# The end of an eight-tile transformer kernel, tile pairs 4-5 and 6-7 handled one after the other

## The reference

```
x = x + attn_a(layernorm(x));  x = x + moe(layernorm(x))
x = x + attn_b(layernorm(x));  x = x + moe(layernorm(x))
x = x + attn_c(layernorm(x));  x = x + ffn(layernorm(x))
x = x + latent_attention(layernorm(x));  x = x + ffn(layernorm(x))
```

```
logits = x @ W_gate.T                       # 8 experts, the top 2 are taken
shared = relu(x @ W_up.T) @ W_down.T
out    = shared + sum(softmax(top2)) * (x @ W_expert)
```

## Time and profile before

| what | value |
|---|---|
| time, median of 3 runs | 1894.64 us (1893.88 to 1895.35) |
| profiled execution, its own time | 1893.86 us |
| its span in the trace | 1892.1 us |
| TensorE busy | 1802.4 us, 95% |
| VectorE busy | 1070.0 us, 57% |
| ScalarE busy | 910.9 us, 48% |
| GpSimd busy | 694.6 us, 37% |
| mean granted TensorE clock | 0.986 of full speed |

### The profile page before, as it was taken

The page is one execution under the profiler, slowest core; times in us unless marked ns, Lnnn a source line. Parts: engine busy times, 40 slices in busy tenths (PEclk is TensorE's granted clock), DMA queues, the critical chain, the costliest instruction groups (busy, mean ns, idle before and its releaser), DMA issues. The chain is left out here.

```text
span 1892.1 us, 30184 instructions
## 1 busy us (share of the span) xinstructions
PE 1802.4 (95%) x10570; PEld 1242.4 (66%) x10580; DVE 1070.0 (57%) x1854; ACT 910.9 (48%) x1938; POOL 694.6 (37%) x627
## 2 busy tenths in 40 slices
PE   6999999999999899999999999899998999999998
PEld 3333688888887555788888887423334677887776
DVE  6776444444445665444444445788864676556544
ACT  3677533333333566433333333468874456445431
POOL 5200466666665110466666664600001345211200
PEclk9799999999999999999999999999999999999999
DMA  4400344444440320354444440490001000000000
GB/s 127 123 1 1 86 121 117 113 112 112 112 102 16 87 81 2 98 125 101 117 116 113 116 123 1 108 181 4 1 1 23 1 1 2 1 1 1 1 12 12
DMA packets 137931, 121.77 MB, mean 64 GB/s; under 512 B 84545, under 2 KB 122905, under 8 KB 137593
## 3 DMA queue, kind: packets, MB, share of 16 engines
q1 hardware_dynamic: 137817, 120.24, 25.5%
HBM read 111.41 MB, written 8.65 MB: 63 GB/s over the span
## 5 line engine op out<-in xcount | busy, mean ns | idle before, releaser
L1418 DVE TENSOR_TENSOR e_inner_lo<-e_inner,e_inner_hi 128x512 fp32r<-128x512 f32 x192 | 244.1, 1271 | 379.2 <-ACT e_inner_hi L1381 379.0
L1404 POOL TENSOR_TENSOR e_wsilu<-e_silu,e_rw 128x512 f32<-128x512 f32 x192 | 262.0, 1364 | 204.3 <-ACT e_silu L1375 186.4
L1351 PE MATMUL psum<-e_x_hi,e_w_hi 128*128 128x512 f32 x768 | 302.5, 394 | 4.7 <-DVE e_inner L1426 4.7
L1351 PE MATMUL psum<-e_x_hi,e_w_lo 128*128 128x512 f32 x768 | 299.2, 390 | 0.0
L1351 PE MATMUL psum<-e_x_lo,e_w_hi 128*128 128x512 f32 x768 | 298.9, 389 | 0.0
L1375 ACT ACTIVATE e_silu<-psum 128x512 f32<-128x512 f32 x192 | 114.7, 597 | 342.6 <-PE psum L1351 342.6
L1413 POOL TENSOR_TENSOR e_w_lo<-e_raw,e_w_hi 128x384 fp32r<-128x384 f32 x180 | 221.1, 1229 | 133.5 <-ACT e_w_hi L1392 121.9
L1351 PEld LDWEIGHTS psum<-e_x_hi,e_w_hi 128*128 128x128 f32 x768 | 144.1, 188 | 44.6 <-DVE e_inner L1426 15.6
L1088 DVE TENSOR_REDUCE c_mx<-psum 128x1 f32<-128x1024 f32 x128 | 150.6, 1219 | 27.4 <-PE psum L957 26.9
L1351 PEld LDWEIGHTS psum<-e_x_hi,e_w_lo 128*128 128x128 f32 x768 | 144.2, 188 | 30.5
L1351 PEld LDWEIGHTS psum<-e_x_lo,e_w_hi 128*128 128x128 f32 x768 | 144.2, 188 | 29.1
(11 more groups left out here) (354 smaller groups left out, 3171.6 us busy)
## 6 DMA issues: line engine op xcount, KB each, us to landing
e_rw<-e_rw_dram SPq DMA_DIRECT2D x56, 384.0 KB, 5.1
e_rw<-e_rw_dram SPq DMA_DIRECT2D x56, 256.0 KB, 5.4
e_raw<-in_L_ffn_w_gate SPq DMA_DIRECT2D x64, 192.0 KB, 2.6
e_raw<-in_L_ffn_w_up SPq DMA_DIRECT2D x64, 192.0 KB, 2.6
e_raw<-in_L_ffn_w_down SPq DMA_DIRECT2D x32, 384.0 KB, 3.6
e_rw<-e_rw_dram SPq DMA_DIRECT2D x72, 128.0 KB, 4.7
e_rw<-e_rw_dram SPq DMA_DIRECT2D x16, 192.0 KB, 3.0
c_parts_dram<-c_part SPq DMA_DIRECT2D x8, 384.0 KB, 2.5
```

Of the source, the lines that this page charges most:

```text
L1351: last = nc.tensor.matmul(bank[u % 2][:], self.w[a][s][:, KC * which + k, j * P:(j + 1) * P], self.x[b][:, k, h * HALF:(h + 1) * HALF], st ...
L1404: self.core.nc.gpsimd.tensor_tensor(self.wsilu[:, u % 2, :], self.silu[:, u % 2, :], self.rw[s][:, j, h * HALF:(h + 1) * HALF], ALU.mult). ...
L1418: self.core.nc.vector.tensor_tensor(self.inner_parts[1][:, u % 3, :], self.inner[:, u % 2, :], self.inner_parts[0][:, u % 3, :], ALU.subtr ...
```

## The change

The work of the end is split by tile pairs.

- In step (15, 6), `invert_part` (VectorE), `inverse_part` (TensorE) and `copy_inverse_part` (ScalarE) handle the inverse row sums of tiles 4 and 5, and VectorE stores the contexts of these two tiles. `values` of step (15, 6) waits for that store.
- `last()` begins with the eighth pair of tiles 4 and 5. It ends with the transposition of their normed rows, ahead of the last `inverse` and `values`. Their residual add and norm stand in VectorE's stream ahead of the last context store, which is now 256 columns wide.
- After the last `values` come up, the eighth pair of tiles 6 and 7, up, route and share. The second pair's turn, route, up and share follow.
- 20 zero matmuls become 4; the 3 others stay. Relu is ScalarE's alone, and banks are given out anew. `hT[1]` moves from `xn` to the spent rotary tables in `xi`.

```diff
@@ LatentAttend @@
+    PART_STEP = (UNITS - 1, HT + 1)
+    def inverse_part(self, pe):
+        key, m = "inverse part", self.PART_STEP[0]
+        pe.wait_ge(self.part_inverted, 2)
+        self.bank_free(pe, key)
+        for t in range(2):
+            last = self.core.nc.tensor.transpose(self.turn_bank(key)[:, t * P:(t + 1) * P], ...
+        last.then_inc(self.turned, 1)
     def values(self, pe, m, t, g):
+        if g == 0 and (m, t) == (self.PART_STEP[0], self.PART_STEP[1] + 1):
+            pe.wait_ge(self.ctx_copied, m + 1)
...
+        if (m, t) == self.PART_STEP:
+            self.inverse_part(pe)
         if t % self.HT == self.HT - 1:
             self.inverse(pe, m)
...
+    def invert_part(self, dve):
+        nc.vector.reciprocal(self.inv_one[:, 0:2, :], self.sums[:, m % 2, 0:2, :]).then_inc(self.part_inverted, 1)
+        dve.wait_ge(self.part_inverted, 1)
+        nc.vector.tensor_copy(self.inv[:, m % 2, 0:2, :, :], ...).then_inc(self.part_inverted, 1)
@@ Second.tensor @@
         def last():
-            latent_out.clear(pe, banks["out"][1])
+            for t in (4, 5):
+                latent_out.project(pe, t, side, range(LPAIRS - 1, LPAIRS), True)
+            latent_out.clear(pe, banks["out"])
             for t in (6, 7):
-                latent_out.project(pe, t, banks["out"][1], range(LPAIRS - 1), True)
+                latent_out.project(pe, t, banks["out"], range(LPAIRS - 1), True)
+            norm.turn_pair(pe, 2, 1, 0, banks["turn"][0])
         latents.tensor(pe, before_part, between, behind, last)
-        for t in range(4, 8):
-            latent_out.project(pe, t, banks["out"][t // 2 - 2], range(LPAIRS - 1, LPAIRS), True)
-        keep_warm(20)
-        norm.turn(pe, 2, 1, banks["turn"])
+        norm.wait_pair_stored(pe, 2, 1, 0)
+        ffn2.up_pair(pe, 2, 0, banks["up"][0])
+        for t in (6, 7):
+            latent_out.project(pe, t, banks["out"], range(LPAIRS - 1, LPAIRS), True)
+        ffn2.up_pair(pe, 2, 1, banks["up"][1])
+        for t in (4, 5):
+            ffn2.route(pe, t, banks["route"][0][t % 2])
+        ffn2.share(pe, 2, banks["share"][0])
+        keep_warm(4)
+        norm.turn_pair(pe, 2, 1, 1, banks["turn"][1])
         keep_warm(3)
-        norm.wait_stored(pe, 2, 1)
-        for m in range(2):
-            ffn2.up(pe, 1, m, banks["up"][m])
-        for t in range(4, 8):
-            ffn2.route(pe, t, banks["route"][t - 4])
-        for n in range(2, 4):
-            ffn2.share(pe, n, banks["share"][n - 2])
+        norm.wait_pair_stored(pe, 2, 1, 1)
+        for t in (6, 7):
+            ffn2.route(pe, t, banks["route"][1][t % 2])
+        for m in range(2):
+            ffn2.up_pair(pe, 3, m, banks["up"][m])
+        ffn2.share(pe, 3, banks["share"][1], 4)
@@ Second.scalar @@
+        latents.scalar(act, behind, lambda: norm.store_pair(act, core.nc.scalar.copy, 2, 1, 0, 0, banks["turn"][0][0]))
+        for m in range(2):
+            ffn2.relu_pair(act, relu, 2, m, banks["up"][m])
+        norm.store_pair(act, core.nc.scalar.copy, 2, 1, 1, 0, banks["turn"][1][0])
+        ffn2.exp(act, 2)
+        ffn2.relu_pair(act, relu, 3, 0, banks["up"][0])
+        ffn2.exp(act, 3)
+        ffn2.relu_pair(act, relu, 3, 1, banks["up"][1])
@@ Second.vector @@
+        def norm_of_pair(p, bank):      # add, gather x2, spread_pair, invert_pair, scale_pair
...
+        latents.vector(dve, behind, before_store)   # before_store: norm_of_pair(0), store(0)
+        norm_of_pair(1, banks["out"])
+        store(1)
+        ffn2.sort(dve, 2, routed)
+        add_routed(2)
+        ffn2.sort(dve, 3, routed)
+        for t in (4, 5):
+            ffn2.add_shared(dve, t, banks["share"][0])
+        add_routed(3)
+        for t in (6, 7):
+            ffn2.add_shared(dve, t, banks["share"][1])
```

More of the change, by code:

```diff
@@ L275, in scale, with pair, spread_pair @@
                                 ALU.subtract, ALU.mult).then_inc(self.normed_v, 1)
+    def pair(self, h, p):
+        return range(4 * h + 2 * p, 4 * h + 2 * p + 2)
+    def spread_pair(self, dve, r, h, p):
+        nc = self.core.nc
+        tiles = self.pair(h, p)
+        for t in tiles:
+            dve.wait_ge(self.gathered[h], 4 * r + t % 4 + 1)
+            nc.vector.bn_aggr(self.mv[:, t, :], self.stats[:, t, :]).then_inc(self.aggregated, 1)
+        dve.wait_ge(self.aggregated, 4 * self.place(r, h) + 2 * p + 2)
+        nc.vector.tensor_scalar(self.var[:, 0, tiles.start:tiles.stop], self.mv[:, tiles.start:tiles.stop, 1], self.EPS, None, ALU.add
+                                ).then_inc(self.varied, 1)
@@ new lines, in scale_pair, with turn_pair @@
+    def scale_pair(self, dve, r, h, p):
+        core = self.core
+        dve.wait_ge(self.inverted, self.place(r, h) + p + 1)
+        for t in self.pair(h, p):
+            core.nc.vector.tensor_scalar(core.xn[:, t, :], core.x[:, t, :], self.mv[:, t, 0:1], self.inv[:, 0, t:t + 1],
+                                         ALU.subtract, ALU.mult).then_inc(self.normed_v, 1)
+    def turn_pair(self, pe, r, h, p, banks):
+        core = self.core
+        for t in self.pair(h, p):
+            pe.wait_ge(self.normed_v, 4 * self.place(r, h) + t % 4 + 1)
+            for k in range(KC):
+                last = core.nc.tensor.transpose(core.bank[banks[k]][:, t % 2 * P:(t % 2 + 1) * P], core.xn[:, t, k * P:(k + 1) * P],
+                                                core.ident[:])
+        last.then_inc(self.turned, 1)
@@ L277, in keep, with store_pair, wait_pair_stored @@
+    def store_pair(self, engine, copy, r, h, p, k, bank):
+        c = h * HALF + p * 2 * P
+        engine.wait_ge(self.turned, self.place(r, h) + p + 1)
+        copy(self.core.xT[:, k, c:c + 2 * P], self.core.bank[bank][:, 0:2 * P]).then_inc(self.copied[k], 1)
+    def wait_pair_stored(self, engine, r, h, p):
+        for k in range(KC):
+            engine.wait_ge(self.copied[k], self.place(r, h) + p + 1)
     def keep(self, t):
@@ L1521, in up, with up_pair, relu_pair, share @@
         last.then_inc(self.up_ready, 1)
-    def share(self, pe, n, bank):
+    def up_pair(self, pe, n, m, bank):
         nc, core = self.core.nc, self.core
-        pe.wait_ge(self.relued[n // 2], 2)
+        for k in range(KC):
+            last = nc.tensor.matmul(core.bank[bank][:, 0:2 * P], core.wup[:, k, m * P:(m + 1) * P],
+                                    core.xT[:, k, 2 * n * P:(2 * n + 2) * P], start=(k == 0), stop=(k == KC - 1))
+        last.then_inc(self.up_ready, 1)
+    def relu_pair(self, engine, relu, n, m, bank):
+        engine.wait_ge(self.up_ready, 2 + 2 * (n - 2) + m + 1)
+        relu(self.hT[1][:, m, n % 2 * 2 * P:(n % 2 + 1) * 2 * P], self.core.bank[bank][:, 0:2 * P]).then_inc(self.relued[1], 1)
+    def share(self, pe, n, bank, relued=2):
+        nc, core = self.core.nc, self.core
+        pe.wait_ge(self.relued[n // 2], relued)
         for t in (2 * n, 2 * n + 1):
@@ L1926, in __init__ @@
                     self.turns[m, t, g, a] = len(self.turns)
+            if (m, t) == self.PART_STEP:
+                self.turns["inverse part"] = len(self.turns)
             if t % HT == HT - 1:
@@ L2167, in invert @@
             dve.wait_ge(self.turned, self.turns["inverse", m - 2] + 1)
+        if m == self.PART_STEP[0]:
+            dve.wait_ge(self.turned, self.turns["inverse part"] + 1)
         nc.vector.reciprocal(self.inv_one[:], self.sums[:, m % 2, :, :]).then_inc(self.inv_made, 1)
@@ L2188, in back @@
                 self.rotate(dve, *part)
-            if t % self.HT == self.HT - 1:
+            if (m, t) == self.PART_STEP:
+                self.store(dve, m, "inverse part", t, slice(0, 2 * P))
+            if (m, t) == self.steps[-1]:
+                before_store()
+                self.store(dve, m, tiles=slice(2 * P, HALF))
+            elif t % self.HT == self.HT - 1:
                 self.store(dve, m)
@@ L2931 @@
               "up0": 12, "up1": 13, "ex0": 13, "ex1": 14, "share0": 14}
-    LAST_BANKS = {"out": (7, 0), "turn": (2, 3), "route": (4, 5, 6, 1), "up": (2, 3), "share": (0, 7)}
+    LAST_BANKS = {"out": 0, "turn": ((1, 2), (6, 7)), "route": ((1, 2), (6, 7)), "up": (3, 5), "share": (4, 0), "zeros": 3}
     def __init__(self, core, c, first_norm, latent):
@@ L3262, in behind, with relu @@
                 ffn2.relu_scalar(act, 0, 1, self.SIDE)
-        latents.scalar(act, behind)
         banks = self.LAST_BANKS
[L3266 to L3269, removed]
+        def relu(dst, src):
+            return core.nc.scalar.activation(dst, src, ACT.Relu)
+        latents.scalar(act, behind, lambda: norm.store_pair(act, core.nc.scalar.copy, 2, 1, 0, 0, banks["turn"][0][0]))
[6 more added lines that the diff above has]
+        ffn2.relu_pair(act, relu, 3, 1, banks["up"][1])
     def vector(self, dve):
@@ L3466, in behind, with store, before_store, add_routed @@
                     ffn2.add_shared(dve, t, self.SIDE)
-        latents.vector(dve, behind)
         banks = self.LAST_BANKS
```

(16 more changed lines are left out.)

57 lines of the change are left out of this document (47 added, 10 removed).

## The result

| | before | changed |
|---|---|---|
| median, first comparison | 1892.5 us (9 runs) | 1888.86 us (1887.22 to 1889.87, 9 runs) |
| ratio, first comparison | | 0.9977, 95% interval 0.9967 to 0.9986 |
| ratio, second and third comparison | | 0.9972 (0.9961 to 0.9982, 8 runs), 0.9981 (0.9972 to 0.9990, 10 runs) |
| profiled execution | 1893.86 us, span 1892.1 | 1889.61 us, span 1887.8 |

The change makes the kernel faster by 0.2 to 0.3%: 4.4 us by the first ratio, 3.6 by the two medians (1892.5 - 1888.86), against a forecast of 4.1. Two of the twelve runs of the third comparison took 7083.43 and 2802.63 us, far above the other ten, and are left out of its figures. The forecast time of 1890.5 and its range from 1889.3 still missed the measured 1888.86. The reason is the starting figure.

A forecast was written before the change was run, and what follows sets the result against it. TensorE's stream was taken as the bound, with one VectorE chain pacing 1867.11 to 1876.98. The last add moves from 1889.41 to 1885.27, 4.14 less, so 1894.64 becomes 1890.5 us; 8-in-10 range 1889.3 to 1892.7.

The forecast's parts named there:

- the last one of the sum: Turning the gain into a median: 0.78 above the profiled execution gives 1894.64, less 4.14 gives 1890.5 us.
- the path's own 1889.7: Low end of the forecast path's range, with 1.1 us lost to the inverse of tiles 4 and 5 and 0.5 won in gaps.
- Part 1: Inverse of tiles 4 and 5 in step (15, 6): its transpositions wait for a bank, 1.36 us lost, bounds 1.1 to 1.9.
- Part 2: `last()`: eighth pair of tiles 4 and 5 and four transpositions add 1.44 us; first norm hidden with 1.2 to spare.
- Part 3: Last `values` to second pair's `xT`: zeros end 0.3 us after VectorE's scaling; route begins at 1878.23, 1.10 later than up before.
- Part 4: Second pair's route to the last add: share loads at 1882.50, end at 1885.27, VectorE with 1.0 us of slack.
- The 2.7 us behind the last add: From the last add to the end of the span, left at 2.7 us as before, the output's DMAs keeping their shape.
- The exposed chain: Rival: VectorE's doubled norm chain shows; with 2.44 us exposed once the time is 1892.9, no change; chance 0.12.
- The clock: Rival: with 16 zeros gone TensorE's clock falls, some 11.5 us more, 1902.0; chance 0.07, of which 0.05 slower.
- Dearer hand-overs: Rival: a dozen engine hand-overs at 0.05 us more, plus the 1.9 bound: 3.0 gained, 1891.6; within the path's 0.80.
- The eighth pair of tiles 4 and 5 didn't wait for the last store: Answers a rival: this eighth pair could still wait for the last store; the prediction held it excluded by the store counts.
- The rule weighed against the change: VectorE pays fixed latency per SBUF-reading instruction, tiles of at least 512 advised; added chain exposed once leaves 1.7 us gained.

The follow-up runs named there:

- before_again: The kernel before, unchanged, timed against itself; ratio 1.0001 (0.9992 to 1.0010).
- up_first_relus: Changed kernel with the second pair's up ahead of its route and both relus ahead of the last exp; last add 42.98 us after step (15, 6)'s row maximum starts.
- no_zeros: Changed kernel without its four and three zero matmuls; last add ends 42.35 us after step (15, 6)'s row maximum starts, against 42.86.
- long_chain: Changed kernel with three spare VectorE multiplications in the first pair's norm; last add ends 42.99 us after step (15, 6)'s row maximum starts, against 42.86.
- best: Changed kernel with the part's transpositions behind the values, no zero matmuls and the last share by halves of the contraction; ratio 0.9966 to the kernel before.
- share_halves: Changed kernel with the last share by halves of the contraction; last add ends 42.33 us after step (15, 6)'s row maximum starts, against 42.86.
- part_only: Kernel before plus only the inverse and store of tiles 4 and 5 in step (15, 6) and the half-width last store; ratio 1.0003.
- part_behind: Changed kernel with the two transpositions of the part's inverse behind the values instead of ahead; ratio 0.9967 to the kernel before.
- part_behind_no_zeros: Changed kernel with the part's transpositions behind the values and no zero matmuls; ratio 0.9969 to the kernel before.

## Why the prediction was wrong, and where it was right

**The step that failed is the last one of the sum, "the median of the runs is 0.78 above that execution, so 1894.64 - 4.14 = 1890.5".** It took a median of three runs as the level, and the range had no term for that: its lower end, 1889.3, lies 0.4 below the path's own 1889.7. The 74 runs of before put the level at 1892.9, and the first comparison, which counts those three, at 1892.5. With 1892.5 the same working gives 1888.4, against the measured 1888.86, and its range moves to 1887.2 to 1890.6. The sizes of the parts, below, didn't put the time outside: with the whole gain of 4.7 taken from 1894.64, the forecast would be 1889.9. That the kernel's level moves between executions is shown by before_again and by the spread of every set. Three places where it moves are shown as well. The first copy of o_ctxT that ScalarE makes starts between 200.3 (before_again) and 203.8 us (up_first_relus), so up to 3.5 us arise ahead of it. The second place lies between the last copy of b_qk and the last of o_ctxT: 127.7 us apart in before (637.9 to 765.6), 129.4 in no_zeros (638.5 to 767.9), and 129.2 in long_chain and in best; all others have 127.6 to 128.1. The stretch from 640 to 700 us in before, with its granted clock third from the right:

```profile
640.00:700.00 60.00, 57.06 (x618) 34.06 (x618) 40.20 (x113) 39.22 (x99) 12.20 (x15) 0.97 0.39 108
```

The same stretch in no_zeros:

```profile
640.00:700.00 60.00, 57.15 (x597) 34.14 (x596) 39.78 (x112) 38.57 (x96) 12.21 (x15) 0.94 0.40 111
```

The 0.94 stands in exactly the three profiles in which this piece is long, no_zeros, long_chain and best; the other eleven have 0.97. With two levels, 1.2 and 2.4 GHz, a mean of 0.94 for 0.97 means 3.6 us more of the 60 at the lower one, which can cost up to 1.8 us of TensorE's work. That is about the size of the 1.1 to 1.8 more.

The first place goes with the clock too: over the first 100 us the mean granted clock is 0.88 in the three profiles that reach o_ctxT first (before_again at 200.3, share_halves at 200.7, part_only at 201.5) and 0.86 in the other eleven (201.9 to 203.8). The third place lies behind the last copy of o_ctxT: from there to M it is 1077.3 us in no_zeros and 1077.4 in best, and the granted clock between 765 and 770 us is 0.72 and 0.66 in these two. Eleven others have 1075.7 to 1076.4 and a clock of 1.00 there. long_chain, with 1074.8 and also 1.00, has no such explanation.

All of this is a correlation over fourteen profiles: no run held the clock fixed, and why the granted clock differs between executions of the same work stays open.

**The mechanism was right, part by part.** Counted from M (the predicted instants less 1842.01):

| instant | predicted | measured |
|---|---|---|
| tile 5's projection | 5.60 | 5.54 |
| last `values` | 25.89 | 25.69 |
| up of the first pair | 27.79 | 27.58 |
| eighth pair of tiles 6 and 7 | 28.65 | 28.34 |
| second turn | 34.75 | 34.43 |
| route of the second pair | 36.22 | 35.82 |
| last share | 40.49 | 40.07 |
| end | 43.26 | 42.86 |

- *Part 1* was sized at 1.36 and cost 1.30. part_only shows this price by itself, and part_behind that the bank wait is most of it.
- *Part 2* was sized at 1.44 and cost 1.30 (25.69 - 5.54, against 18.85 before). The eighth pair of tiles 4 and 5 took 0.73 and not 0.86. Its cover, put at 1.2 of slack, was 1.5 in long_chain.
- *Part 3* took 0.2 less than its 10.33 (36.22 - 25.89): up took 0.76, from 1870.00 to 1870.76, and not 0.86, and from the second turn to route it was 1.39 and not 1.47. The zeros and not VectorE held the second turn, as predicted, but by 0.5 and not 0.3: in no_zeros the copy behind the turn starts 34.78 after M (1879.94 - 1845.16) and not 35.29 (1877.71 - 1842.42).
- *Part 4* took 7.04 where 7.04 was predicted (43.26 - 36.22, 42.86 - 35.82). Its exactness is luck: route and up took 3.38 and not 3.52 (1878.24 to the end of up's loads at 1881.62), and the wait for the relu behind them was 0.88 and not 0.75, since the relu began 0.44 and not 0.28 behind the loads. VectorE's slack, put at 1.0, shows as 1.08 of idle.
- *The 2.7 us behind the last add* became 2.5. The two output transfers were issued 0.66 apart before and 3.7 apart now, so the last one now has the DMA engines for itself, which may be the reason; it isn't shown. I had left this as it was before.

One reading of the kernel before was wrong without cost to the sum: that TensorE sets the pace from 1877.13 until the last adds end. From 1884.40 on VectorE did, as its timeline above shows. The sum took the end of before as measured and built the new one from both engines, so it stands; but the most that the change could win was not TensorE's work alone.

Together the forecast gain of 4.14 was 4.54 up to the last add and 4.7 to the end of the span, counted from M: the misses in parts 1, 2 and 3 and behind the last add all went to the same side. That is inside the forecast's own range of gains and no miss of mechanism. The profile's absolute end, predicted at 1885.27 and measured at 1885.28, is a coincidence: M was 0.41 later than in the profile of before, and the end 0.40 shorter than predicted.

**The rivals.** The exposed chain falls by long_chain for the first norm and by the 1.08 that VectorE waits at the end; the second norm stays covered only by the four zeros (no_zeros). The clock falls by no_zeros. Dearer hand-overs fall by the table, except for the one from up to relu. The eighth pair of tiles 4 and 5 didn't wait for the last store: its loads begin at 1859.91, and that store at 1870.12. The rule weighed against the change, of the Trainium skill ("VectorE: DVE Perf Modes", the section on the TRN2 errata), is borne out as a price by the Newton steps, which read SBUF: they take 0.16 us each for two columns as they did for four, and start 0.20 apart in both. Two 256-column copies take 0.84 where one of 512 took 0.69, but they read PSUM and don't test that sentence. The rule does not decide, since the first chain lies under TensorE's records, and the second shows, by 0.43, only when the zeros are gone.

## What to carry to other kernels

Before forecasting an absolute time, look how far the shown runs spread and whether they are few; forecast the difference from a landmark, and give the level a term of its own in the range. For a short tail, compare distances from one instruction that both kernels share: they repeated to 0.05 us where the program's time moved by 2 to 4. Follow VectorE to the very end of the kernel as well: an engine that is busy 57% on average can still end it. When an item is inserted into an alternation of banks, look for whose copy it now waits and put it behind work that covers that wait; here moving two transpositions won 1.1 us of the 1.3 that they had cost.

## What the runs showed that I had not expected

- The same work ahead of o_ctxT's first copy took up to 3.5 us more or less from execution to execution, while the 418 us behind it (to the first copy of b_qk) repeated within 417.3 to 418.4 in all fourteen profiles.
- TensorE kept 2.4 GHz through the end without any zero matmul, with 0.8 us without a weight load ahead of route and 0.9 ahead of the last share (no_zeros, part_behind_no_zeros).
- Four fp32 load records of 256-column matmuls took 0.73 us where other kinds of loads ran ahead of them (at 1859.91 and 1870.00 in the changed kernel) and 0.84 behind their own kind (1870.76). The 0.216 each from long groups gives 0.86.
